# A fused attention stack: norm product in two column tiles, its least square laid on the sums in PSUM, roots spread by transfers

## The chip, the cores and the metric

One core of a Trainium2 chip runs the whole kernel in one launch. The metric is the device time of an execution in microseconds. Engines: PE is the tensor engine (PEld its weight loads), DVE the vector engine, ACT the scalar engine, POOL GpSimd, SP the engine whose queue issues the transfers.

## What is computed

The input x is (8, 256, 128) in float32. It is layer-normalised, and the result is x plus two branches of the normalised rows. The first is causal attention with 16 heads of 64. The second has six layers of local attention (window 32) and a gated MLP, and the part of it that matters here is the normalisation of queries and keys:

```python
def l2norm(t):
    return t / jnp.maximum(jnp.linalg.norm(t, axis=-1, keepdims=True), 1e-12)
...
q = l2norm(q) * qs
k = l2norm(k) * ksc
q = q * cos * scale + rotate_half(q) * sin * scale
k = k * cos * inv + rotate_half(k) * sin * inv
out = local_attention(q, k, v)
```

`qs` and `ksc` are per-channel factors, cos, sin and scale depend on the position alone. So the kernel multiplies the raw projections with tables that hold the factors and the positions, and applies 1/norm per token and head afterwards.

## The kernel before, in words

**Units, groups, slots.** A unit is one of the 8 batch rows in one of the 6 layers, so there are 48 units. Each has 4 groups of 4 heads; a group m has its place in a stream of 192 groups (`GROUPS`). The program of every engine is a loop over slots s, from -4 to a few past 192 (`slot(s)` in each engine's block), and in one slot the engines work on different groups: the projections and rotation are those of group s+4, the norm product that of s+3, the scores and softmax those of s, the weighting of the values that of s-1, the output projection that of s-2. The order within a slot is written out by hand for each engine, each engine runs it in order, and semaphores join them. The first four slots (-4 to -1) run inside the last batch of the causal branch. The MLP of two units together is spread over the slots 13 to 21 of a cycle of 8 slots (`mlp_slot`), so a slot's extra work depends on s modulo 8. Layer boundaries, every 32 slots, add weight loads, weight splits on POOL (L426, L431) and, on ACT, new rotary tables (L643).

**The norm of queries and keys.** In a slot:
- PE projects K (`keys`, L1061 to L1063, first half) and, later in the slot, Q (`queries`) of group s+4 into the banks `B_K` and `B_Q`, as three single-pass products each half.
- DVE multiplies each with the tables (`rotate`: L1376 into `rot_u`, L1377 into `rot_v`); ACT squares each (`squares`, L655 into `sq`). For Q, DVE waits until ACT has squared (it waits for `q_square`); for K, ACT waits for DVE (`k_prod`).
- POOL adds `rot_u` and the swapped `rot_v` (`rotated`, L442, into `z_raw`, one operation for K and one for Q) and the two halves of the squares (L469, into `sqs`, 128x512: K and Q by 256 tokens).
- PE multiplies `sqs` (group s+3) with the matrix `blk`, 128x128, ones where both indices lie in the same block of 32 (`norms`, L1010, 512 columns): every partition of `B_N` then holds the sum of squares of its own head. The operands are float32, which takes two passes of PE for a product, two records in the trace.
- ACT takes Ln (L735) and Exp with the scale -0.5 (L738), both 128x512, so that `rinv` is the reciprocal root, on all partitions.
- DVE clips it to 1e12 (L1458, `bound_ready`), after the softmax weights of the slot.
- POOL multiplies `z_raw` with it (`normalise`, L436, once for K and once for Q) into `z_norm`. Its order: rotated K (s+4), normalise K (s+3), sum of squares (s+4), normalise Q (s+3), rotated Q (s+4).
- SP moves `z_norm` of group s+2 into `zqk` (L365, four transfers of 128 KB) with the layout of the scores, and then part of the values into `v_late` (L371, L372, group s+3).

**The softmax and the rest of the slot.** PE makes the scores (`windows`, L1029) onto a mask that ACT (L689) or PE (L1020) has laid into `pair_bank`. DVE: maximum (L1355), shift (L1357), rotation of K (L1376, L1377), then, after ACT's Exp (L731), sum (L1362), reciprocal (L1364) and weights (L1367), then the clip L1458, then MLP products (L1419) and residuals (L1411), then the rotation of Q. In some slots it begins with L1349 (spreading), L1391 (MLP residual) or L1398 (a copy for the layer norm). ACT: values out of PSUM (L595), spreading (L664), Exp of the scores (L731), Ln and Exp of the norms (L735, L738), `yt` (L696), squares of K, pieces of layer norm and MLP (L684, L678, L702), the mask (L689), squares of Q. In the slot of remainder 1 the mask stands ahead of the squares of K. PE: transposes of the weights (L1039), scores, K projection, output projection (L978), norm product, weighting of the values (L1051, in column tiles of 64), an MLP product (L1113, L1127 or L1135), Q projection, V projection (L1073 to L1075), and in some slots products for the layer norm (L1149, L1157). The V projection overwrites `B_N`, so it waits for ACT's Ln.

Of the kernel before, what the change touches and what calls it, by code (L numbers as in the profile page):

```python
# [16 lines left out]
P = 128  # L17
# [45 lines left out]
for _name, _n in (("ident", P), ("mask_causal", P), ("mask_local", 4 * KEYS), ("blk", P),  # L63
                  ("center", P), ("avg", P), ("rot", 4 * T)):
    CONST[_name] = (_at, _n)
    _at += _n
# [3 lines left out]
def constants():  # L70
# [17 lines left out]
    put("blk", i // 32 == np.arange(P)[None, :] // 32)  # L88
# [14 lines left out]
def build(nc, x, w_kv_down, w_kv_up, w_q, w_out, Wqkv, q_scale, k_scale, Wo, ln_g, ln_b, W1, b1, W2, b2, const, out):  # L103
    with ExitStack() as ctx:
# [42 lines left out]
        z_raw = sb("z_raw", [P, 2, 2, 2, T])  # L147
        z_norm = sb("z_norm", [P, 2, 2, 2, T])
# [7 lines left out]
        x_rows = z_norm.rearrange("p g a b t -> p (g a b t)").rearrange("p (n c) -> p n c", c=P)  # L156
        xn_rows = z_raw.rearrange("p g a b t -> p (g a b t)").rearrange("p (n c) -> p n c", c=P)
# [4 lines left out]
        late_ln = probs.rearrange("p h c -> p (h c)")[:, 2 * GW * 2:].rearrange("p (a t) -> p a t", a=2)  # L162
        late_rinv = probs_t.rearrange("p h c -> p (h c)")[:, 2 * GW * 2:].rearrange("p (a t) -> p a t", a=2)
# [13 lines left out]

        def ln_n(m):

            return late_ln if m >= G else gate[:, 0:2, 0:T]  # L180

        def rinv(m):

            return late_rinv if m >= G else gate[:, 0:2, T:2 * T]
# [16 lines left out]
            n_done ln_done rinv_ready bound_ready zn_ready z_in0 z_in1 z_in2 z_in3 lv_ready v_late_in0 v_late_in1 v_late_in2 v_late_in3  # L201
# [81 lines left out]
        def _(sp):  # L283
# [72 lines left out]
            def slot(s):  # L356
                if active(s, -2, GROUPS - 2):
# [5 lines left out]
                    for pair in range(2):  # L363
                        for half in range(2):
                            sp.dma_start(zqk[half:P:2, g, :, pair, :], z_norm[64 * pair:64 * pair + 64, s % 2, :, half, :]).then_inc(S[f"z_in{g}"], 16)  # L365
                if active(s, -3, GROUPS - 3):

                    g, odd = (s + 3) % G, (s + 3) // G % 2
                    cols = slice(g * GW, (g + 1) * GW)
                    sp.wait_ge(S["lv_ready"], s + 4)  # L370
                    sp.dma_start(v_late[WIN:P, odd, :, cols], v_sb[0:P - WIN, odd, :, cols]).then_inc(S[f"v_late_in{g}"], 16)  # L371
                    sp.dma_start(v_late[0:WIN, odd, 1, cols], v_sb[P - WIN:P, odd, 0, cols]).then_inc(S[f"v_late_in{g}"], 16)  # L372
# [40 lines left out]
        def _(pool):  # L413
# [19 lines left out]
            def normalise(m, idx):  # L433

                parity = m % 2
                return pool.tensor_tensor(z_norm[:, parity, idx, :, :], rinv(m)[:, idx, :].unsqueeze(1).broadcast_to([P, 2, T]), z_raw[:, parity, idx, :, :], ALU.mult)  # L436

            def rotated(m, parity, idx, prod, mark):

                pool.wait_ge(S[prod], m + 1)  # L440
                after(pool, "zn_ready", m - 1)
                pool.tensor_tensor(z_raw[:, parity, idx, :, :], rot_u[:, idx, :, :], rot_v[:, idx, ::-1, :], ALU.add).then_inc(S[mark], 1)  # L442
# [8 lines left out]
            def slot(s):  # L451
                g = s % G
                one, two = active(s, -4, GROUPS - 4), active(s, -3, GROUPS - 3)
# [3 lines left out]
                if one:  # L457
                    rotated(s + 4, s % 2, 1, "k_prod", "k_summed")
                if two:

                    pool.wait_ge(S["bound_ready"], s + 4)
                    after(pool, f"z_in{(s + 1) % G}", 16 * HG * ((s + 1) // G + 1))
                    pool.wait_ge(S["k_summed"], s + 4)
                    normalise(s + 3, 1)
# [5 lines left out]
                if two:  # L470
# [1095 lines left out]
```

## Time and profile before

| | before |
|---|---|
| time, median of 3 runs | 1865.2 us (1863.66 to 1868.27) |
| the profiled execution's own time | 1865.6 us |
| its span, first to last instruction | 1863.8 us |
| busy: PE, DVE, ACT, POOL | 1804.9, 1531.7, 1455.7, 1359.5 us |
| mean granted clock of PE | 0.998 |
| share of 16 DMA engines, SP's queue | 35.9% |

The span is that of the profiled execution, whose own time is 1.8 us longer. Busy times overlap between engines. In a timeline row stand start, duration, engine, line, operation, output<-input, shape and count, and in brackets the idle time of the engine before it with its releaser. Starts of two neighbouring instructions on DVE and ACT lie some 0.1 us closer together than the first one's duration, so their starts, not their durations, are what adds up along a queue.

### The profile page before, as it was taken

To read this page: it belongs to the slowest core of one execution; us is meant where nothing else is said; L and a number is where in the kernel's file an instruction comes from. 1 tells how busy PE (TensorE), PEld (TensorE's weight loads), DVE (VectorE), ACT (ScalarE), POOL (GpSimd) and SP (SyncE) were. 2 spreads that over 40 slices of the span, in tenths; PEclk is the share of its full clock that TensorE was granted. 3 is DMA by queue.
4 is the path that set the end of the run, shared out by engine and by line. 5 is a ranking of instruction groups with operands and counts; after the bars stand their busy time and mean duration, and the time that the engine had idled before them with its cause. 6 is when DMAs were issued, how large, how long until landed. Compare 5 with 4: busy or idle time off the path is not lost.

```text
span 1863.8 us, 67159 instructions
## 1 busy us (share of the span) xinstructions
PE 1804.9 (97%) x26763; PEld 1367.6 (73%) x26763; DVE 1531.7 (82%) x3002; ACT 1455.7 (78%) x2976; POOL 1359.5 (73%) x1165
## 2 busy tenths in 40 slices
PE   6999998999999999999999999999999999999997
PEld 4777776777777777777777777777777777777774
DVE  5776777788889888888888888888888888888886
ACT  5766665688788878888887888878878888887884
POOL 3010033899889888888888898889888888888880
PEclk9999999999999999999999999999999999999999
DMA  3000001344444444444443444444444444444342
GB/s 111 1 1 0 0 25 38 96 123 115 101 101 115 106 112 104 100 112 103 119 110 97 104 111 111 115 107 101 105 110 109 114 99 107 112 103 100 95 106 64
DMA packets 188251, 170.91 MB, mean 92 GB/s; under 512 B 20112, under 2 KB 187192, under 8 KB 187960
## 3 DMA queue, kind: packets, MB, share of 16 engines
q1 hardware_dynamic: 187960, 166.84, 35.9%
q8 instruction: 206, 3.38, 0.8%
q14 instruction: 85, 0.70, 0.1%
HBM read 21.01 MB, written 1.05 MB: 12 GB/s over the span
## 4 chain that ended last, share of the span: by engine, by line
PE 65%; ACT 12%; DVE 11%; issue 7%; POOL 4%; DMA 0%; SPq 0%; ACTq 0%; POOLq 0%; DVEq 0%
PE bank L1010 6%; PE bank L1051 6%; PE bank L978 6%; PE pair_bank L1029 5%; PE bank L1061 4%; PE bank L1113 3%; PE bank L1062 3%; PE bank L1063 3%; PE bank L1039 3%; PE bank L1135 3%; PE bank L896 2%; ACT sq L655 2%; DVE rot_v L1377 2%; ACT probs L735 2%; DVE rot_u L1376 2%
## 5 line engine op out<-in xcount | busy, mean ns | idle before, releaser
L436 POOL TENSOR_TENSOR z_norm<-probs_t,z_raw 128x512 f32<-128x512 f32 x376 | 480.9, 1279 | 101.2 <-DVE probs_t L1458 101.2
L442 POOL TENSOR_TENSOR z_raw<-rot_u,rot_v 128x512 f32<-128x512 f32 x384 | 498.3, 1302 | 70.8 <-DVE rot_v L1377 69.6
L1376 DVE TENSOR_TENSOR rot_u<-bank,tabs 128x512 f32<-128x512 f32 x384 | 262.9, 685 | 175.9 <-ACT sq L655 174.5
L1061 PE MATMUL bank<-x_high,w_high 128*128 128x256 f32 x768 | 302.1, 393 | 0.0
L469 POOL TENSOR_TENSOR sqs<-sq 128x512 f32<-128x512 f32 x192 | 246.3, 1283 | 60.5 <-issue 59.3
L1377 DVE TENSOR_TENSOR rot_v<-bank,tabs 128x512 f32<-128x512 f32 x384 | 261.1, 680 | 0.0
L1051 PEld LDWEIGHTS bank<-probs_t,v_late 128*64 128x64 f32 x3072 | 155.0, 137 | 144.5 <-issue 144.5
L655 ACT ACTIVATE sq<-bank 128x512 f32<-128x512 f32 x384 | 222.1, 593 | 24.1 <-PE bank L1063 17.7
L731 ACT ACTIVATE pair_bank<-pair_bank 128x512 f32<-128x512 f32 x192 | 111.7, 582 | 165.0 <-DVE pair_bank L1357 163.4
L664 ACT ACTIVATE probs_t<-bank 64x512 f32<-64x512 f32 x340 | 200.8, 591 | 22.7 <-PE bank L1039 20.7
L1063 PE MATMUL bank<-x_low,w_high 128*128 128x256 f32 x768 | 216.3, 282 | 0.0
L1062 PE MATMUL bank<-x_high,w_low 128*128 128x256 f32 x768 | 216.1, 281 | 0.0
L1010 PE MATMUL bank<-sqs,consts 128*128 128x512 f32 x384 | 197.6, 596 | 9.9 <-POOL sqs L469 9.9
L1051 PE MATMUL bank<-probs_t,v_late 128*64 128x64 f32 x3072 | 198.8, 228 | 0.5 <-ACT probs_t L664 0.5
L978 PE MATMUL bank<-yt,wo 128*128 128x256 f32 x768 | 197.8, 380 | 0.0
L1051 PE MATMUL bank<-probs_t,v_sb 128*64 128x64 f32 x3072 | 189.5, 222 | 0.0
L1061 PEld LDWEIGHTS bank<-x_high,w_high 128*128 128x128 f32 x768 | 144.6, 188 | 58.0 <-issue 38.5
L1062 PEld LDWEIGHTS bank<-x_high,w_low 128*128 128x128 f32 x768 | 145.8, 190 | 36.9 <-issue 36.9
L735 ACT ACTIVATE probs<-bank,tiny 128x512 f32<-128x512 f32 x188 | 129.1, 686 | 43.6 <-PE bank L1010 41.9
L1029 PE MATMUL pair_bank<-zqk 64*32 64x64 f32 (+1 forms) x12288 | 161.4, 221 | 0.9
L1051 PEld LDWEIGHTS bank<-probs_t,v_sb 128*64 128x64 f32 x3072 | 156.0, 138 | 0.0
L1029 PEld LDWEIGHTS pair_bank<-zqk 64*32 64x32 f32 x12288 | 130.6, 105 | 34.7 <-issue 34.7
(190 smaller groups left out, 4533.9 us busy)
## 6 DMA issues: line engine op xcount, KB each, us to landing
zqk<-z_norm SPq DMA_DIRECT2D x768, 128.0 KB
v_late<-v_sb SPq DMA_DIRECT2D x192, 192.0 KB, 2.6
w_stage<-in_L_ffn_Wqkv SPq DMA_DIRECT2D x24, 384.0 KB, 3.6
v_late<-v_sb SPq DMA_DIRECT2D x192, 32.0 KB, 2.2
wo<-in_L_ffn_Wo SPq DMA_DIRECT2D x24, 128.0 KB, 2.4
w<-in_L_ffn_W SPq DMA_DIRECT2D x12, 170.5 KB, 2.7
z_norm<-in_L_attn_x SPq DMA_DIRECT2D x4, 256.0 KB, 5.0
out<-z_raw SPq DMA_DIRECT2D x4, 256.0 KB, 2.3
```

The lines of the kernel that those rows point to most:

```text
L436: return pool.tensor_tensor(z_norm[:, parity, idx, :, :], rinv(m)[:, idx, :].unsqueeze(1).broadcast_to([P, 2, T]), z_raw[:, parity, idx, : ...
L442: pool.tensor_tensor(z_raw[:, parity, idx, :, :], rot_u[:, idx, :, :], rot_v[:, idx, ::-1, :], ALU.add).then_inc(S[mark], 1)
L655: act.activation(sq[:, idx, :, :], src[:, :].rearrange("p (a t) -> p a t", a=2), ACT.Square).then_inc(S[mark], 1)
L978: mm = pe.matmul(B_X[:, 0:T], wo[:, c, :], yt[:, c, :], start=(c == 0), stop=(c == HD // P - 1))
L1010: pe.matmul(B_N[:, :], con("blk"), sqs[:, :, :].rearrange("p a t -> p (a t)"), start=True, stop=True).then_inc(S["n_done"], 1)
L1029: mm = pe.matmul(bank[a][WIN * tile:WIN * tile + WIN, at + skip:at + KEYS], zqk[rows, g, 0, pair, WIN * j:WIN * j + WIN], zqk[rows, g, 1, ...
L1051: mm = pe.matmul(y[:, t, tile % 2, :, :], (v_sb if tile % 2 else v_late)[:, odd, t, f], spread[:, h, tile, :], start=True, stop=True, tile ...
L1061: pe.matmul(dst, w_high[:, r, j, cols], x_high[:, odd, :], start=True, stop=False)
L1062: pe.matmul(dst, w_low[:, r, j, cols], x_high[:, odd, :], start=False, stop=False)
L1063: mm = pe.matmul(dst, w_high[:, r, j, cols], x_low[:, odd, :], start=False, stop=True)
L1376: dve.tensor_tensor(rot_u[:, idx, :, :], src, tabs[:, 2 * idx, :, :], ALU.mult)
L1377: dve.tensor_tensor(rot_v[:, idx, :, :], src, tabs[:, 2 * idx + 1, :, :], ALU.mult).then_inc(S[mark], 1)
```

## The change

It has four parts.
- **The norm product** gives each head's sum on 16 partitions instead of 32: `blk` is 128x64, and two products of 256 columns put K's or Q's sums on partitions 0 to 63 (the first, idx 0, which is Q) and 64 to 127 (the second, K) of the first 256 columns of `B_N`, in two column tiles of PE (`tile_position` (0, 0) and (0, 64)).
- **The least square**: DVE lays max(sum, 1e-24) on the sums in `B_N`, in place, 128x256, in place of the clip of the root. It stands in DVE's slot right after the rotation of K, ahead of the softmax weights, and waits for the norm product. ACT's Ln waits for it. Ln and Exp run over 128x256.
- **The root is spread by transfers**: a new group of four transfers by SP writes the 64 rows of each root to all 128 partitions of a buffer `wide` (every second partition, twice, for Q and for K; 64 KB each). They stand at the head of SP's slot behind the `v_late` transfers, which move ahead of the `z` transfers.
- **Normalising** happens a slot later (group s+2 instead of s+3), in place in one buffer `z` of four groups, which replaces `z_raw` and `z_norm`. POOL's order is now: rotated K (s+4), normalise K and Q (s+2), sum of squares (s+4), rotated Q (s+4). The transfers into `zqk` still leave in slot s for group s+2.

```diff
-    put("blk", i // 32 == np.arange(P)[None, :] // 32)
+    put("blk", i // 32 == np.arange(P // 2)[None, :] // 16)
...
-        z_raw = sb("z_raw", [P, 2, 2, 2, T])
-        z_norm = sb("z_norm", [P, 2, 2, 2, T])
+        z = sb("z", [P, G, 2, 2, T])
...
+        def wide(m):
+            return (late_wide if m >= G else early_wide)[:, m % 2, :, :]
...
@@ SP, slot(s) @@
+                if active(s, -3, GROUPS - 3):
+                    g, odd = (s + 3) % G, (s + 3) // G % 2
+                    cols = slice(g * GW, (g + 1) * GW)
+                    sp.wait_ge(S["lv_ready"], s + 4)
+                    sp.dma_start(v_late[WIN:P, odd, :, cols], v_sb[0:P - WIN, odd, :, cols]).then_inc(S[f"v_late_in{g}"], 16)
+                    sp.dma_start(v_late[0:WIN, odd, 1, cols], v_sb[P - WIN:P, odd, 0, cols]).then_inc(S[f"v_late_in{g}"], 16)
+                    sp.wait_ge(S["rinv_ready"], s + 4)
+                    after(sp, "zn_ready", s + 2)
+                    for idx in range(2):
+                        for k in range(2):
+                            sp.dma_start(wide(s + 3)[k:P:2, idx, :], rinv(s + 3)[64 * idx:64 * idx + 64, :]).then_inc(S[f"wide_in{(s + 3) % 2}"], 16)
                 if active(s, -2, GROUPS - 2):
...
-                            sp.dma_start(zqk[half:P:2, g, :, pair, :], z_norm[64 * pair:64 * pair + 64, s % 2, :, half, :]).then_inc(S[f"z_in{g}"], 16)
-                if active(s, -3, GROUPS - 3):
...
+                            sp.dma_start(zqk[half:P:2, g, :, pair, :], z[64 * pair:64 * pair + 64, g, :, half, :]).then_inc(S[f"z_in{g}"], 16)
...
@@ POOL @@
+                zs = z[:, m % G, idx, :, :]
+                return pool.tensor_tensor(zs, wide(m)[:, idx, :].unsqueeze(1).broadcast_to([P, 2, T]), zs, ALU.mult)
...
-                after(pool, "zn_ready", m - 1)
+                after(pool, f"z_in{m % G}", 16 * HG * (m // G))
...
-                if two:
-
-                    pool.wait_ge(S["bound_ready"], s + 4)
-                    after(pool, f"z_in{(s + 1) % G}", 16 * HG * ((s + 1) // G + 1))
-                    pool.wait_ge(S["k_summed"], s + 4)
-                    normalise(s + 3, 1)
+                if near:
+                    pool.wait_ge(S[f"wide_in{s % 2}"], 16 * HG * ((s + 2) // 2 + 1))
+                    pool.wait_ge(S["k_summed"], s + 3)
+                    normalise(s + 2, 1)
+                    pool.wait_ge(S["q_summed"], s + 3)
+                    normalise(s + 2, 0).then_inc(S["zn_ready"], 1)
...
@@ ACT @@
-                    act.wait_ge(S["n_done"], m + 1)
-                    act.activation(ln_n(m), B_N[:, :].rearrange("p (a t) -> p a t", a=2), ACT.Ln, bias=tiny[:, 0:1], scale=LNS).then_inc(S["ln_done"], 1)
+                    act.wait_ge(S["bound_ready"], m + 1)
+                    after(act, f"wide_in{m % 2}", 16 * HG * (m // 2))
+                    act.activation(ln_n(m), B_N[:, 0:T], ACT.Ln, bias=tiny[:, 0:1], scale=LNS).then_inc(S["ln_done"], 1)
...
-                    after(act, "zn_ready", m)
...
@@ PE @@
-                pe.matmul(B_N[:, :], con("blk"), sqs[:, :, :].rearrange("p a t -> p (a t)"), start=True, stop=True).then_inc(S["n_done"], 1)
+                for idx in range(2):
+                    rows = slice(64 * idx, 64 * idx + 64)
+                    mm = pe.matmul(B_N[rows, 0:T], con("blk"), sqs[:, idx, :], start=True, stop=True, tile_position=(0, 64 * idx), skip_group_check=True)
+                mm.then_inc(S["n_done"], 1)
...
@@ DVE, slot(s) @@
                     rotate(s + 4, 1, B_K, "lk_done", "k_summed", "k_prod")
+                if two:
+                    dve.wait_ge(S["n_done"], s + 4)
+                    dve.tensor_scalar(B_N[:, 0:T], B_N[:, 0:T], 1e-24, None, ALU.max).then_inc(S["bound_ready"], 1)
...
                     weigh_down(s)
-                if two:
-                    dve.wait_ge(S["rinv_ready"], s + 4)
-                    dve.tensor_scalar(rinv(s + 3), rinv(s + 3), 1e12 / ROOT, None, ALU.min).then_inc(S["bound_ready"], 1)
```

## Rows read from the trace of the kernel before

**Rows 1.** Page, part 1: busy time and share of the span.
```profile
PE 1804.9 (97%) x26763; PEld 1367.6 (73%) x26763; DVE 1531.7 (82%) x3002; ACT 1455.7 (78%) x2976; POOL 1359.5 (73%) x1165
```

**Rows 2.** Timeline of PE: scores of slots 16, 96, 99, 100, 104, 184.
```profile
448.75 0.68 PE L1029 MATMUL pair_bank<-zqk 64*32 64x32 f32 x47
...
1084.48 0.84 PE L1029 MATMUL pair_bank<-zqk 64*32 64x32 f32 x64
...
1107.10 0.84 PE L1029 MATMUL pair_bank<-zqk 64*32 64x32 f32 x64
...
1114.91 0.84 PE L1029 MATMUL pair_bank<-zqk 64*32 64x32 f32 x64
...
1147.18 0.84 PE L1029 MATMUL pair_bank<-zqk 64*32 64x32 f32 x64
...
1780.34 0.68 PE L1029 MATMUL pair_bank<-zqk 64*32 64x32 f32 x48
```

**Rows 3.** Timeline of DVE, slot 103 (r = 7).
```profile
1139.00 0.69 DVE L1376 TENSOR_TENSOR rot_u<-bank,tabs 128x512 f32<-128x512 f32 x1 [1.50 <-ACT sq L655]
...
1140.20 0.41 DVE L1398 COPY xc<-bank 128x256 f32<-128x256 f32 x1
1140.54 0.68 DVE L1355 TENSOR_REDUCE nm<-pair_bank 128x8 f32<-128x512 f32 x1
...
1142.46 0.68 DVE L1377 TENSOR_TENSOR rot_v<-bank,tabs 128x512 f32<-128x512 f32 x1
...
1144.00 0.69 DVE L1367 TENSOR_TENSOR probs<-pair_bank,rrec 128x512 f32<-128x512 f32 x1
...
1147.03 0.69 DVE L1376 TENSOR_TENSOR rot_u<-bank,tabs 128x512 f32<-128x512 f32 x1 [2.00 <-ACT sq L655]
```

**Rows 4.** Timeline of PE around one norm product.
```profile
1007.11 1.02 PE L1010 MATMUL bank<-sqs,consts 128*128 128x512 f32 x2
...
1008.07 0.34 PE L1051 MATMUL bank<-probs_t,v_late 128*64 128x64 f32 x4
...
1009.15 1.12 PE L1113 MATMUL bank<-xh,w 128*128 128x512 f32 x2
```

**Rows 5.** Groups by line, 700 to 1400 us: count, busy, mean, idle.
```profile
L1458 DVE TENSOR_SCALAR probs_t<-probs_t 128x512 f32<-128x512 f32 x88 | 49.9, 567 | 0.0
...
L670 ACT ACTIVATE ln_v<-bank,tiny 128x256 f32<-128x256 f32 x22 | 10.4, 474 | 0.6
```

**Rows 6.** Timeline of ACT, slot 103 (r = 7).
```profile
1142.80 0.69 ACT L735 ACTIVATE probs<-bank,tiny 128x512 f32<-128x512 f32 x1 [0.24 <-PE bank L1010]
...
1144.06 0.58 ACT L696 ACTIVATE yt<-bank 128x512 f32<-128x512 f32 x1
...
1145.02 0.41 ACT L684 ACTIVATE xc<-xc 128x256 f32<-128x256 f32 x1
1145.32 0.68 ACT L702 ACTIVATE gate<-bank,gate_bias 85x512 f32<-85x512 f32 x1
1145.89 0.59 ACT L689 ACTIVATE pair_bank<-mask_local_b 128x512 f32<-128x512 bf16 x1
1146.41 0.59 ACT L655 ACTIVATE sq<-bank 128x512 f32<-128x512 f32 x1
```

**Rows 7.** Timeline of DVE, slots of remainder 1, 2, 5.
```profile
900.92 1.38 DVE L1349 COPY probs_t<-bank 64x512 f32<-64x512 f32 x2
...
1105.17 0.74 DVE L1419 SCALAR_TENSOR_TENSOR hid<-bank,out_bias,gate 128x512 f32<-128x512 f32 x1
...
1124.83 1.51 DVE L1391 SCALAR_TENSOR_TENSOR xs<-bank,out_bias,xs 64x512 f32<-64x512 f32 x2
```

**Rows 8.** Timeline of ACT, slot 100 (r = 4): squares of Q.
```profile
1122.99 0.60 ACT L655 ACTIVATE sq<-bank 128x512 f32<-128x512 f32 x1 [1.27 <-PE bank L1063]
```

**Rows 9.** Timeline of SP, slot 100: a group's `z` and values.
```profile
1116.93 3.48 SPq L365 DMA_DIRECT2D zqk<-z_norm  x4
1120.46 0.64 SPq L371 DMA_DIRECT2D v_late<-v_sb  x1
```

More of the change, by code:

```diff
@@ L62 @@
 _at = 0
-for _name, _n in (("ident", P), ("mask_causal", P), ("mask_local", 4 * KEYS), ("blk", P),
+for _name, _n in (("ident", P), ("mask_causal", P), ("mask_local", 4 * KEYS), ("blk", P // 2),
                   ("center", P), ("avg", P), ("rot", 4 * T)):
@@ L153, in build @@
         nm = sb("nm", [P, HG, TT])
-        x_rows = z_norm.rearrange("p g a b t -> p (g a b t)").rearrange("p (n c) -> p n c", c=P)
-        xn_rows = z_raw.rearrange("p g a b t -> p (g a b t)").rearrange("p (n c) -> p n c", c=P)
+        z_rows = z.rearrange("p g a b t -> p (g a b t)").rearrange("p (n c) -> p n c", c=P)
+        x_rows, xn_rows = z_rows[:, 0:NB * TT, :], z_rows[:, NB * TT:2 * NB * TT, :]
         probs = sb("probs", [P, HG, 3 * P])
@@ L176, in build @@
         causal_stage = [w_stage] + [a.rearrange("p (j n) -> p j n", j=3) for a in (hid_flat[:, 0:3 * GW], hid_flat[:, 3 * GW:6 * GW], gate_flat[:, 0:3 * GW])]
+        early_wide = gate_flat[:, 0:4 * T].rearrange("p (q a t) -> p q a t", q=2, a=2)
+        early_rows = gate_flat[:, 4 * T:6 * T].rearrange("p (q t) -> p q t", q=2)
         def ln_n(m):
-            return late_ln if m >= G else gate[:, 0:2, 0:T]
+            return rinv(m)
         def rinv(m):
-            return late_rinv if m >= G else gate[:, 0:2, T:2 * T]
+            return (late_rows if m >= G else early_rows)[:, m % 2, :]
+        def wide(m):
+            return (late_wide if m >= G else early_wide)[:, m % 2, :, :]
         pair_bank = ctx.enter_context(nc.psum_tensor("pair_bank", [P, 2, 512], F32))
@@ L433, in normalise, with rotated @@
             def normalise(m, idx):
-                parity = m % 2
-                return pool.tensor_tensor(z_norm[:, parity, idx, :, :], rinv(m)[:, idx, :].unsqueeze(1).broadcast_to([P, 2, T]), z_raw[:, parity, idx, :, :], ALU.mult)
-            def rotated(m, parity, idx, prod, mark):
+                zs = z[:, m % G, idx, :, :]
+                return pool.tensor_tensor(zs, wide(m)[:, idx, :].unsqueeze(1).broadcast_to([P, 2, T]), zs, ALU.mult)
+            def rotated(m, idx, prod, mark):
                 pool.wait_ge(S[prod], m + 1)
-                after(pool, "zn_ready", m - 1)
-                pool.tensor_tensor(z_raw[:, parity, idx, :, :], rot_u[:, idx, :, :], rot_v[:, idx, ::-1, :], ALU.add).then_inc(S[mark], 1)
+                after(pool, f"z_in{m % G}", 16 * HG * (m // G))
+                pool.tensor_tensor(z[:, m % G, idx, :, :], rot_u[:, idx, :, :], rot_v[:, idx, ::-1, :], ALU.add).then_inc(S[mark], 1)
             def split_input(unit, b, odd):
@@ L452, in slot @@
                 g = s % G
-                one, two = active(s, -4, GROUPS - 4), active(s, -3, GROUPS - 3)
+                one, near = active(s, -4, GROUPS - 4), active(s, -2, GROUPS - 2)
                 if s == 0:
@@ L469, in slot @@
                     pool.tensor_tensor(sqs[:, :, :], sq[:, :, 0, :], sq[:, :, 1, :], ALU.add).then_inc(S["sums_ready"], 1)
-                if two:
-                    pool.wait_ge(S["q_summed"], s + 4)
-                    normalise(s + 3, 0).then_inc(S["zn_ready"], 1)
-                if one:
-                    rotated(s + 4, s % 2, 0, "q_prod", "q_summed")
+                    rotated(s + 4, 0, "q_prod", "q_summed")
                 if g == 0 and active(s, -4, GROUPS - 8):
@@ L1455, in slot @@
                     weigh_down(s)
-                if two:
-                    dve.wait_ge(S["rinv_ready"], s + 4)
-                    dve.tensor_scalar(rinv(s + 3), rinv(s + 3), 1e12 / ROOT, None, ALU.min).then_inc(S["bound_ready"], 1)
                 if s == 0:
```

13 lines of the change are left out of this document (4 added, 9 removed).

## The prediction

> **What bounds the kernel now.** I read first the busy shares: TensorE (PE) is busy for 1804.9 of 1863.8 us, 97%, the vector engine (DVE) for 82%, ScalarE (ACT) for 78%, POOL for 73% [rows 1]. Then the starts of the score matmuls (L1029) give the length of slots; I number slots by their remainder r by 8, since the MLP comes round every 8. One such group of 8 slots without a layer boundary takes 1147.18 - 1084.48 = 62.70 us; slots 16 to 184 take 1331.6 us, 63.41 per group, so layer boundaries add 0.71 per group, 14.9 us over the 21 groups [rows 2]. PE's timeline has hardly a gap inside a slot. DVE and ACT do wait: in a slot of r = 7 DVE stands idle 2.00 us until the squares of Q are done [rows 3]. So PE is the bound, and the question is how much slack the ring between DVE and ACT has, since the change lengthens it.
>
> **Part 1: norm product in two column tiles.** The product with `blk` (L1010) takes PE from 1007.11 to 1008.07, 0.96 us for two passes of 512 columns; of this I take 0.10 for the change to column tiles behind it (an estimate), 0.43 for a pass [rows 4]. The new one has 256 columns in each of two tiles. Nearest rows: the 32 passes of L1051, 64 columns each in tiles of 64, go in 1.08 us (1008.07 to 1009.15), 34 ns a pass [rows 4]. At L1010's rate (0.43 us for 512 columns) one pass of 64 columns takes 54 ns, so two tiles run side by side. Then the four new passes of 256 take 2 x 0.215 = 0.43 us instead of 0.86; the 0.10 of the change to column tiles moves ahead of the product and stays. PE gives back 0.43 us a slot. Bounds: 0.43 and 0 (tiles one after the other). The Trainium skill has a rule against it: TensorE: Matmul & The Clock Gate, Part 3 (The mechanism), says that a weight load overlaps matmuls in flight only where the row group differs, and the two tiles here share all rows. By that rule the product would keep near its 0.86 us and the time be the 1895 of rival B; L1051's tiles share their rows too and do overlap, so the row speaks against the rule.
>
> **Part 2: the bound (1e-24) laid on the sums by DVE, before ACT's Ln.** Today ACT goes from its Exp of the scores straight to Ln (it needs the norm product alone), and DVE's bound (L1458, mean 567 ns [rows 5]) comes after the softmax weights. The new bound is a 128x256 operation on PSUM; the nearest row, the 128x256 copy out of PSUM (L1398), took 0.41 and the next instruction started 0.34 after it [rows 3]. I take 0.34 for it in the queue; L1458's mean for 512 columns in SBUF [rows 5] gives both ends, half of it and the whole: 0.28 and 0.57, less the same 0.07 of overlap 0.21 and 0.50. The page VectorE: DVE Perf Modes, Why PSUM operands drop a tier (the Trainium skill), says that fp32 with a PSUM operand runs at the plain rate; L1398 agrees, and by it the low end falls away.
> ACT's Ln and Exp shrink to half the width: from Ln's start to the start of `yt` was 1144.06 - 1142.80 = 1.26 [rows 6]; a Ln of 128x256 took 474 ns [rows 5], 0.50 to the next start, and an ACT operation of 128x256 (L684) took 0.41, of which 0.33 is queue: 0.83.
> But Ln now waits for DVE, in whose queue stand the reduce of the scores, the shift, the two K rotations, and then the bound. Take N, the start of the reduce L1355 at 1140.54. The second K rotation ends at 1142.46 + 0.68 = 1143.14, N+2.60 [rows 3]; the bound ends at N+2.94, Ln starts at N+2.98 and `yt` at N+3.81. Without the wait Ln would follow the scores' Exp. Queued behind Ln on ACT stand Exp, `yt`, squares of K, MLP pieces, the mask and the squares of Q; for the last DVE waits before it rotates Q, and behind that stands the next slot's reduce. That closes the ring.
>
> **Its length.** After `yt` starts ACT needs, at r = 7, 1147.00 - 1144.06 = 2.94 until the squares of Q end; of this L684 is 0.30, the gate bias L702 0.57, the mask L689 0.52, the last squares 0.59 [rows 6]. Without MLP pieces Q = 2.07, without the mask too 1.55. Then 0.03 to DVE's rotation of Q and 1.20 until DVE is free for the next [rows 3]. A step from N to the next N is so 3.81 + Q + 1.23 + E = 5.04 + Q + E; E is what DVE does first: 0.34 for L1398 (r = 3, 7), 1.41 for the two L1349 (r = 1), 1.54 for the two L1391 (r = 5) [rows 3, 7].
> - r = 0: 5.04 + 1.55 + 1.41 = 8.00.
> - r = 1: the mask comes before the squares and needs the softmax weights, at N + 2.94 + 1.55 = 4.49 (L1367 ends 1.55 after the rotation [rows 3]): 4.53 + 0.52 + 0.48 + 0.59 + 1.23 + 0 = 7.36.
> - r = 5: 7.11. r = 6: 5.04 + 2.64 + 0.34 = 8.02. r = 7: 5.04 + 2.94 = 7.98.
> - r = 2 to 4: here PE is in the chain. The hidden product (L1419) ends at N + 4.49 + 0.67 = 5.16; from its end to the score matmuls of r = 3 is 1107.10 - 1105.91 = 1.19; that slot takes PE 7.81 - 0.43 = 7.38 [rows 2, 7]; from the scores of r = 4 to the end of the squares of Q, behind the down-projection, 1123.59 - 1114.91 = 8.68, less 0.43 = 8.25 [rows 2, 8]; then 0.03 + 1.20 + 1.54. Sum 24.75. (The ring alone would give 24.0.)
> Together 63.22 us against 62.70, while PE's own work falls to 62.70 - 8 x 0.43 = 59.3. In the old order `yt` started at 1144.06 - 1140.54 = N+3.52, and that with ACT waiting for PE's product ahead of Ln, so the ring was 0.3 us a slot shorter or more and stood hidden behind PE. Over 21 groups +0.52 makes +10.9 us.
>
> **The rest.** Layer boundaries: the old 14.9 us came in good part from L1458 held up while POOL splits weights (its mean of 567 ns is above L1398's 0.41 [rows 3, 5]), with POOL's norm behind it; the new bound is in PSUM and POOL no longer waits for it, so I drop them. In their place the rotary tables (L643) stand in ACT's queue before the squares: two and some small copies at r = 3, four at r = 4, each 128x256 as L684 with its 0.41 [rows 6], an estimate of 1.1 and 1.6 us. Of these 2.7 PE's lead at the down-projection (8.25 against the ring) hides 0.7; the stretch r = 2 to 4 grows by 2.0, x 5 layers = +10. Weight splits on POOL ahead of `sqs` and the bias copy: an estimate of 0.6 a layer, +3. The first 16 slots have a ring with few extras: +2. POOL keeps its five operations (73% busy in all [rows 1]) and stays hidden while slots keep their length; its sum of squares comes one operation later, and without that cover PE's product would be late. SP issues per slot two `v_late`, the four new transfers of 64 KB and four `z`, in that order. One issue takes 0.64, ten 6.4; the four `z` took 3.48, so 0.9 of stall [rows 9], together 7.3 of 7.9 us: hidden, with 0.6 to spare; if that goes, rival C. The norms a slot later, in place, cost nothing: the `z` transfers leave in the same slot as before, the rest is waits met long ago.
> Sum: +10.9 - 14.9 + 10 + 3 + 2 = +11 on the profiled execution's own 1865.6 us (span 1863.8), which is 0.4 above the median: **1877 us**.
>
> **Rivals.** A (the other side): PE stays the bound, and its 0.43 x 192 = 82 us come out: 1784. For it: PE is at 97% and DVE and ACT show idle time [rows 1, 3]. Against it: that idle time is the slack that the new wait uses up. It decides if the ring is under 59.3 a group, 0.5 us less in each slot than I sum; anything between scales (0.3 less would give 1827). Chance 0.15.
> B: the tiles don't overlap. The two 0.43 in the stretch r = 2 to 4 are then not saved: 0.86 x 21 = +18, 1895. Chance 0.10.
> C: SP becomes the bound: if the new transfers show the stall of 0.9 too, SP needs 8.2 a slot, 65.6 a group, +50 and more; where only some slots do, 1890 to 1930. Chance 0.13.
> My forecast, the DVE-ACT ring: 0.62. Its own range comes from the bound, which stands six times in a group: 0.13 less each is -16, 0.16 more +20, which the rest doesn't add to in full, and rounding of some 40 terms, +/-8: 1857 to 1897.
>
> **Numbers.** A measurement of this kernel can tell about 0.3%, 5.6 us, from no change. The range takes in the forecast's, B and the lower part of C: 1855 to 1905; left out are A and half of C. Faster: A and a little of the forecast's low end, 0.19. Same: 0.18 of the forecast. Slower: the rest, 0.63.
>
> **What would show it.** After: slots of some 7.9 us as before; PE's busy share down to about 94%; its norm product 0.43 us; PE waiting ahead of the scores and the mask; Ln (L735 before) with about 0.9 us idle before it, released by the bound; DVE still waiting for the squares. Wrong, if slots shrink to 7.4 with PE closed up (A), if the product takes 0.86 (B), or if `z` or the roots land late (C).

## The result and the profile after

The changed kernel takes **1894.12 us** (median of 4 runs, 1893.61 to 1895.13) against 1864.68 (median of 4 runs of before on the same chip, 1863.66 to 1868.27): ratio 1.0155, 95% interval 1.0137 to 1.0173. The forecast was 1877 us with a range of 1855 to 1905: slower as forecast, but by 29 us where the sum gave 11 (12 against the median of before). The profiled execution has a span of 1892.8 us against 1863.8.

First the page: part 1 and the chain that ended last (part 4).

```profile
PE 1755.7 (93%) x27147; PEld 1362.9 (72%) x27147; DVE 1528.6 (81%) x3002; ACT 1371.9 (72%) x2976; POOL 1354.5 (72%) x1165
...
DVE 34%; PE 32%; ACT 14%; issue 11%; SPq 5%; DMA 1%; POOL 1%; ACTq 0%; DVEq 0%
```

PE went from 97% [rows 1] to 93%, and the chain is no longer PE's: DVE holds a third of it, and PE's share fell from 65% to 32%. The waits name the ring (the engine that waits and its line, the line waited for: us in total, times, longest):

```profile
DVE rot_u L1386 <- ACT sq L662: 212.8, 146, 2.5
...
ACT probs_t L743 <- DVE bank L1464: 168.8, 187, 0.9
...
PE pair_bank L1039 <- DMA zqk<-z: 8.2, 12, 1.3
```

ACT's Ln (L743) waits 0.9 us in nearly every slot for DVE's bound (L1464), and DVE waits for ACT's squares of Q. PE's waits for `z` are small. The starts of the score matmuls (L1039; slots 0, 16, 96, 104, 184), to set beside [rows 2]:

```profile
338.78 0.84 PE L1039 MATMUL pair_bank<-zqk 64*32 64x32 f32 x64
...
460.38 0.81 PE L1039 MATMUL pair_bank<-zqk 64*32 64x32 f32 x62
...
1103.30 0.85 PE L1039 MATMUL pair_bank<-zqk 64*32 64x32 f32 x64
...
1166.93 0.85 PE L1039 MATMUL pair_bank<-zqk 64*32 64x32 f32 x64
...
1809.25 0.84 PE L1039 MATMUL pair_bank<-zqk 64*32 64x32 f32 x64
```

A group of 8 slots without a layer boundary takes 63.63 us (1166.93 - 1103.30), 62.70 before. Slot 0 of before, which the rows ahead of the prediction lack, starts so:

```profile
332.01 1.11 PE L1029 MATMUL pair_bank<-zqk 64*32 64x32 f32 x64
```

So the 29.0 us by which the span grew divide into **start** 338.78 - 332.01 = +6.8; **first 16 slots** 121.60 against 116.74 = +4.9; **slots 16 to 184** 1348.87 against 1331.59 = +17.3; behind them +0.1.

One slot of r = 0 (slot 104). Timeline of DVE, answering to [rows 3]:

```profile
1170.51 0.42 DVE L1464 TENSOR_SCALAR bank<-bank 128x256 f32<-128x256 f32 x1
1170.84 1.39 DVE L1413 TENSOR_TENSOR xc<-xc,rstd 128x256 f32<-128x256 f32 x1
1172.16 0.68 DVE L1372 TENSOR_REDUCE rsum<-pair_bank 128x8 f32<-128x512 f32 x1
...
1173.71 0.68 DVE L1386 TENSOR_TENSOR rot_u<-bank,tabs 128x512 f32<-128x512 f32 x1
```

Timeline of POOL in the same slot:

```profile
1170.67 1.28 POOL L453 TENSOR_TENSOR z<-rot_u,rot_v 128x512 f32<-128x512 f32 x1 [1.25 <-DVE rot_v L1387]
1171.91 2.68 POOL L447 TENSOR_TENSOR z<-probs,z 128x512 f32<-128x512 f32 x2
```

Timeline of ACT there, answering to [rows 6]:

```profile
1170.97 0.47 ACT L743 ACTIVATE probs_t<-bank,tiny 128x256 f32<-128x256 f32 x1 [0.95 <-DVE bank L1464]
...
1172.28 1.07 ACT L662 ACTIVATE sq<-bank 128x512 f32<-128x512 f32 x2
```

Timeline of PE around the product, answering to [rows 4]:

```profile
1169.48 0.65 PE L1019 MATMUL bank<-sqs,consts 128*64 128x256 f32 x4
1169.97 0.28 PE L1061 MATMUL bank<-probs_t,v_late 128*64 128x64 f32 x4
```

The bound takes 0.33 us in the queue (1170.51 to 1170.84; I took 0.34). The next instruction is the product that gives the MLP's normed rows (L1413, "the late norms" below; L1403 before). It takes 1.39 us; in most slots of before it took 0.41 (mean of all 1269 ns, 610 before). POOL had started its K sum (L453) 0.17 us before it, and the product ends 0.28 us after that operation (1171.95). Of the 48 of these products in each of the two kernels, every one that began while a POOL operation ran ends 0.28 to 0.31 us after that operation. In most slots of before either no POOL operation ran there, or one that ended some 0.12 us after the product's start, and so it took 0.41. The squares of Q are done at 1173.35, but DVE comes to the rotation of Q only at 1173.71.

### The profile page after: what moved, and what is told of

Its sections match the earlier page's. It is cut to its first block, busy times and chain, and to the rows that moved or that the text cites. A ratio compares the mean times of both kernels' runs of the same rounds, so it can differ in the third digit from the quotient of the medians.

```text
span 1892.8 us, 68880 instructions
## 1 busy us (share of the span) xinstructions
PE 1755.7 (93%) x27147; PEld 1362.9 (72%) x27147; DVE 1528.6 (81%) x3002; ACT 1371.9 (72%) x2976; POOL 1354.5 (72%) x1165
## 4 chain that ended last, share of the span: by engine, by line
DVE 34%; PE 32%; ACT 14%; issue 11%; SPq 5%; DMA 1%; POOL 1%; ACTq 0%; DVEq 0%
DVE rot_u L1386 9%; DVE rot_v L1387 9%; ACT sq L662 5%; DVE nm L1365 5%; DVE bank L1464 3%; ACT yt L703 2%; PE bank L1145 2%; SPq L383 2%; ACT pair_bank L696 2%; PE bank L1061 2%; PE bank L903 2%; ACT probs_t L743 2%; PE bank L985 2%; SPq L374 2%; DVE rsum L1372 2%
## 5 line engine op out<-in xcount | busy, mean ns | idle before, releaser
L453 POOL TENSOR_TENSOR z<-rot_u,rot_v 128x512 f32<-128x512 f32 x384 | 491.0, 1279 | 234.6 <-DVE rot_v L1387 234.6
L447 POOL TENSOR_TENSOR z<-probs,z 128x512 f32<-128x512 f32 x376 | 480.8, 1300 | 3.6 <-DMA probs<-probs_t 3.5
L743 ACT ACTIVATE probs_t<-bank,tiny 128x256 f32<-128x256 f32 x188 | 89.1, 474 | 168.8 <-DVE bank L1464 168.8
L985 PE MATMUL bank<-yt,wo 128*128 128x256 f32 x768 | 197.7, 380 | 0.0
L1061 PEld LDWEIGHTS bank<-probs_t,v_late 128*64 128x64 f32 x3072 | 173.3, 138 | 33.1 <-issue 9.3
L1061 PE MATMUL bank<-probs_t,v_late 128*64 128x64 f32 x3072 | 190.7, 222 | 1.8 <-ACT probs_t L671 1.6
L1039 PE MATMUL pair_bank<-zqk 64*32 64x64 f32 (+1 forms) x12288 | 165.1, 221 | 17.6 <-ACT pair_bank L696 9.4
L1039 PEld LDWEIGHTS pair_bank<-zqk 64*32 64x32 f32 x12288 | 134.5, 105 | 53.3 <-issue 40.7
L1049 PE MATMUL bank<-consts,probs 128*128 128x128 f32 x768 | 117.9, 276 | 31.1 <-DVE probs L1377 29.3
```

Of the source, the lines that this page charges most:

```text
L447: return pool.tensor_tensor(zs, wide(m)[:, idx, :].unsqueeze(1).broadcast_to([P, 2, T]), zs, ALU.mult)
L453: pool.tensor_tensor(z[:, m % G, idx, :, :], rot_u[:, idx, :, :], rot_v[:, idx, ::-1, :], ALU.add).then_inc(S[mark], 1)
L985: mm = pe.matmul(B_X[:, 0:T], wo[:, c, :], yt[:, c, :], start=(c == 0), stop=(c == HD // P - 1))
L1039: mm = pe.matmul(bank[a][WIN * tile:WIN * tile + WIN, at + skip:at + KEYS], zqk[rows, g, 0, pair, WIN * j:WIN * j + WIN], zqk[rows, g, 1, ...
L1061: mm = pe.matmul(y[:, t, tile % 2, :, :], (v_sb if tile % 2 else v_late)[:, odd, t, f], spread[:, h, tile, :], start=True, stop=True, tile ...
```

## The experiments

Two theories stand against each other: **R**, the ring between DVE and ACT through the bound sets the pace; **C**, SP's ten issues a slot and the transfers behind them do. The recorded expectations call C also "S" or "SP theory", and P stands there for PE as the bound. Where nothing else is said, line numbers are the changed kernel's. Each run stands beside runs of before on its chip, medians 1864.25 to 1865.78.

### The order alone

The kernel before, with `B_N` bounded at full width behind the rotation of K, Ln waiting for it, and the clip of the root (L1458 before) gone: no transfers, no column tiles.

> The kernel before with one part of the change alone: DVE lays max(sum, 1e-24) on the sums in PSUM right after the rotation of K, here over all 512 columns, and ACT's Ln waits for it; the clip of the root is left out. Full-width product, Ln and Exp, no new transfers, the norms in their old slot. Theory R (the ring between DVE and ACT sets the length of a slot): the bound takes about 0.60 us of DVE's queue and Ln with Exp 1.26, so a step of the ring is 5.73 us + Q + E instead of 5.04 + Q + E, a group of 8 slots 67 to 69 us, and the time 1960 to 2010 us. Rival S (the cost lies in the transfers, SP's queue and the norms a slot later): none of these is here, the time stays near 1865, at most 1875 us. Rival P (PE is the bound and the tiles are the cause): near 1865 too.

**2003.57 us** (one run), a group 68.3 us, both as R had them. The bound in this place, at double width, makes the old kernel 139 us slower with not one transfer more.

### The old clip put back

In short form (Ln waits for the product alone again):

```
-  dve: wait n_done; B_N[:, 0:T] = max(B_N[:, 0:T], 1e-24)     (ahead of Ln)
+  dve: wait rinv_ready; rinv = min(rinv, 1e12 / ROOT)         (behind the weights; SP waits for it)
```

> The changed kernel with that one part undone: Ln waits for the norm product alone, and DVE clips the root (now 128x256) after the softmax weights, as before the change; SP's transfers of the root wait for the clip. Tiles, half width, transfers and the norms a slot later stay. R: the ring is back under PE's work, a group takes 59.3 to 60 us, the time is 1780 to 1800 us, and Ln has hardly any idle time before it that DVE ends. S: the transfers and the moved norms are still there, so it stays at 1880 or above. P (the tiles save PE nothing): about 1865 us.

**1913.18 us**, ratio 1.0253 (1.0233 to 1.0272). For R, which gave 1780 to 1800, that is a miss of over 110 us; C had 1880 or above. Its groups between slots 16 and 184 are irregular, 64.2 to 67.4 us. The chain of its page:

```profile
PE 32%; DVE 32%; SPq 12%; issue 12%; ACT 6%; DMA 5%; POOL 1%; ACTq 0%; DVEq 0%
```

One of its waits (total, times, longest; in the changed kernel it was 12.3 us in 17 times):

```profile
PEld pair_bank L1039 <- DMA zqk<-z: 43.9, 67, 3.1
```

Its clip, by form (count, busy, mean ns, idle before): late slots, then the first four:

```profile
L1468 DVE TENSOR_SCALAR probs_t<-probs_t 128x256 f32<-128x256 f32 x188 | 219.0, 1165 | 3.4 <-ACT probs_t L745 3.4
L1468 DVE TENSOR_SCALAR gate<-gate 128x256 f32<-128x256 f32 x4 | 1.6, 406 | 1.6 <-ACT gate L745 1.6
```

With the ring open two costs show at once. The clip, both sides in SBUF, takes 1165 ns on the mean. POOL, which in the old order waited for it, now works beside it: 183 of the 192 clips last over 0.5 us, and each of them began during a POOL operation and ends 0.14 to 0.16 us after it. The seven that began with POOL idle took 0.28 us (three of the first four, whose mean of 406 ns holds one late one). And SP waits for the clip, then issues late; `z` lands late, and PE waits. R is not refuted, but C stands right behind it.

### The product twice; the first four groups free

```
-  for idx in range(2):            (L1019, norm product)
+  for idx in (0, 1, 0, 1):
```

> The changed kernel with the norm product issued twice (four column-tile products instead of two, same result). The added 0.43 us of PE in each slot: under R PE is in the chain only in the stretch from remainder 2 to 4, for two slots of it, so a group grows by 0.86 us and the time by 18 to 24 us, to 1912 to 1918. If PE were the bound everywhere, by 0.43 x 192 = 82 us, to 1976. If nothing of PE were in the chain, by nothing. If the tiles ran one after the other, the product would add 0.86 a slot, 36 us or more under R.

**1910.37 us** (one run), +16; a group 64.5 us, 0.8 more. It lies just under R's 1912 to 1918, and far from the 1976 of a PE that is the bound everywhere: 0.8 us a group is the added product in two slots of eight, which fits the prediction's stretch r = 2 to 4.

```
-  if two:                         (bound of DVE)
+  if two and s + 3 >= G:
```

and Ln of the first four groups waits for the product alone: this kernel leaves out their least square.

> The changed kernel, but in the first four groups (those worked on inside the last batch of the causal branch) Ln waits for the product alone and their least square is left out. R: there PE's V projection waits up to 3.6 us four times, since Ln waits for a bound that stands in DVE's queue behind the causal softmax; with it gone the first scores of the local attention start at about 332 us instead of 338.8, PE's granted clock from 300 to 340 us is back above 0.9 from 0.79, and the time is 6 to 8 us less, about 1887. S: no difference beyond 2 us, since the transfers stay.

**1890.94 us** (one run), -3.2, where 6 to 8 less were expected. The start came back whole: first scores at 331.0 instead of 338.8. The rest of the run lost some 4 us again (steady groups 63.9, not 63.6; ACT has one more wait in each slot, the likely reason, not tested). The clock shows what had happened at the start. Windows, changed kernel; columns: window, its length, busy us of PE, PEld, DVE, ACT, POOL, mean granted clock of PE, DMA share and GB/s:

```profile
300.00:320.00 20.00, 12.72 (x80) 9.22 (x81) 11.33 (x33) 9.37 (x33) 5.17 (x5) 0.77 0.10 26
320.00:340.00 20.00, 16.36 (x159) 11.71 (x158) 10.71 (x29) 9.64 (x29) 11.73 (x10) 0.80 0.35 83
```

and this run:

```profile
300.00:320.00 20.00, 15.73 (x116) 10.56 (x114) 13.84 (x40) 12.54 (x42) 9.02 (x8) 1.00 0.16 41
320.00:340.00 20.00, 17.23 (x183) 12.70 (x188) 12.32 (x28) 8.47 (x24) 12.00 (x11) 0.91 0.37 90
```

In the changed kernel PE stands idle for 3.64 us before its V projection three times (0.78 to 0.93 in the kernel before), and the granted clock has a mean of 0.77 and 0.80 of the full 2.4 GHz in the two stretches, so PE ran part of them at the lower level, 1.2 GHz. In this run two waits of 0.71 are left of them, and the clock is 1.00 and 0.91, as in the kernel before. The row is the changed kernel's:

```profile
319.45 0.58 PE L1083 MATMUL bank<-w_high,x_high 128*128 128x256 f32 x1 [3.64 <-ACT gate L743]
```

### The bound ahead of the rotation of K; the late norms ahead of the bound

Only the order of DVE's blocks is changed in each.

> The changed kernel, with the bound on the sums put ahead of DVE's rotation of K instead of behind it (nothing left out). Ring theory: Ln then starts about 0.9 us earlier after the reduce of the scores, so the ring is shorter than PE's work (some 60 us for a group of 8 slots); without another bound the time falls to 1795 to 1830 us, PE's share of the span rises over 95%, and Ln waits no more than about 0.3 us a slot. SP theory: with that wait gone, the issue of ten transfers a slot and the stall of each (some 7.3 to 8.2 us a slot) sets the pace: 1840 to 1885 us, with PE waiting for zqk from the transfers as in the run with the clip put back. If neither: the rotation of K, now later, delays POOL and the squares of K, and the time stays at 1885 to 1900.

**1897.31 us**, ratio 1.0174 (1.0153 to 1.0194): the third case. Its DVE:

```profile
614.37 0.70 DVE L1367 TENSOR_TENSOR pair_bank<-pair_bank,nm 128x512 f32<-128x512 f32 x1
616.01 0.43 DVE L1462 TENSOR_SCALAR bank<-bank 128x256 f32<-128x256 f32 x1 [0.94 <-PE bank L1019]
616.35 0.68 DVE L1386 TENSOR_TENSOR rot_u<-bank,tabs 128x512 f32<-128x512 f32 x1
```

The norm product stands behind the scores, the K projection and L985 in PE's order and ends 3.0 us into the slot. The bound then waits 0.94 for it with the rotation of K, the sums and the softmax weights queued behind. In this slot Ln starts 2.83 us after the scores' reduce, 2.98 in the changed kernel, and the sums (L1372) 3.90 after it, 2.86 there: little gained for Ln, 1.0 lost for the rest. As means of slots 16 to 184 Ln gains 0.59 and the sums lose 0.31. The rotation of K had filled that wait of DVE. The loss comes back in the ring, for ACT's mask now waits for the softmax weights (7.8 us in all in the changed kernel):

```profile
ACT pair_bank L696 <- DVE probs L1377: 100.0, 140, 1.5
```

> The changed kernel with one thing moved: the product that gives the normed rows (1.40 us in the slots of remainder 0 and 4, 0.41 in the kernel before) stands ahead of the bound instead of behind it. If it is long because POOL's rotated K holds the SBUF port just then, it goes back to about 0.4 us, and the bound then comes 0.4 later: the step of slot r = 0 stays near 8.3 us, and the time within 6 us of the changed kernel (1888 to 1900). If it is long by its own form, it stays at 1.4 us and delays the bound: +1 us in two slots of 8, 1915 us and more.

**1899.89 us** (one run); the product fell to a mean of 480 ns (1269 in the changed kernel), steady group 63.7. As expected (1888 to 1900), and no gain: 0.33 of bound and product change places in the ring. So it is not long by its own form. (The 6 us more lie in the first 16 slots, 127.9 us against 121.6; their cause is open.)

### Without the bound

> The changed kernel with the least square left out: Ln waits for the norm product alone. Ring theory: the ring between DVE and ACT is open, and PE is the bound again with 0.48 us less a slot: 1784 to 1805 us. SP theory: ten transfers a slot set the pace, 1840 to 1885 us, with waits of PE for zqk. The difference between this run and the one with the bound first is what the bound costs when it is early: by the ring theory under 15 us.

**1838.48 us**, ratio 0.9859 (0.9838 to 0.988). So the bound costs 56 us in all, and taking it away makes the kernel 26 us faster than before. But it doesn't reach PE's 1784 to 1805: what is left is C's, just under the 1840 that it gave.

> The changed kernel with the least square as the bias of ACT's Ln (sum + 1e-24 in place of the larger of the two; Ln had a bias already) and DVE's instruction gone: no instruction is left for the bound and Ln waits for the norm product alone. It has the schedule of the run without a bound, so every theory gives that run's time: 1832 to 1845 us. If it differs, Ln's time depends on the bias.

The edit: `tiny[:, 0:1]` = LNS * 1e-24 (2^-64 before), which Ln adds to LNS times the sum. **1840.93 us**, ratio 0.9882 (0.9865 to 0.99), as expected. Its chain:

```profile
PE 37%; SPq 32%; DVE 10%; ACT 7%; issue 7%; DMA 4%; POOL 2%; ACTq 0%; DVEq 0%
```

and its SP in one slot, from one L368 to the next, 7.92 us, of which issues take 7.69:

```profile
612.94 0.64 SPq L368 DMA_DIRECT2D v_late<-v_sb  x1
613.62 0.62 SPq L369 DMA_DIRECT2D v_late<-v_sb  x1
614.34 2.46 SPq L374 DMA_DIRECT2D probs<-probs_t  x4
616.84 3.97 SPq L383 DMA_DIRECT2D zqk<-z  x4
620.86 0.64 SPq L368 DMA_DIRECT2D v_late<-v_sb  x1
```

Four new transfers take 2.46, the four `z` 3.97, so 1.5 us of stall in this slot (3.07 and 0.6 in the one before). This is a full slot; as a mean of slots 16 to 184 the ten issues take 6.9 us (6.0 to 8.9) of 7.7.

> The kernel before with its bound moved in the same way (bias of Ln, DVE's L1458 gone, POOL's normalise waits for the root alone). PE is the bound there at 97%: inside a group nothing changes; DVE's held up L1458 at the layer boundaries goes, worth at most the 15 us that they add: 1850 to 1863 us. If the bound held the old kernel back elsewhere too, under 1845.

**1844.80 us**, ratio 0.9895 (0.988 to 0.9909): below what I expected. PE holds 85% of the chain, and the steady group is 62.2 us, not 62.7: in the old kernel too, DVE's clip held up the hidden product in the slots of r = 2 (8.46 us, now 8.00). So most of what the version with the bound as a bias gains has nothing to do with this change: the two differ by 4 us, with intervals that overlap. What PE gives back with 0.48 us a slot is not seen in the time, since SP's queue is next (see the added issue below).

### Who issues, and how often

> As the run with the bound ahead of the rotation of K, and besides the four transfers that spread the root are issued on ACT's queue instead of SP's, right behind the Exp that makes the root (ACT waits there for its own Exp to be written, and issues four). SP theory: SP is free of four of ten issues and of the wait for the root, so if SP was the bound, the time falls by 20 us or more against that run. Ring theory: ACT's four issues (an estimate of 0.05 to 0.6 us each in its queue) stand between the Exp and the square root pieces of the next slot; at 0.6 each the ring is 2.4 us longer and the time goes over 1950; at 0.1 each it stays within 15 us of that run.

**2360.33 us**, ratio 1.267. That is over 1950, as R had it for long issues: four of them take ACT 2.41 us, in the ring. Against the run with the bound first it is 463 us more, and 192 x 2.41 is 463 too; PE's mean granted clock is 0.92 here, and what that adds was not parted from it.

```profile
800.18 2.41 ACTq L745 DMA_DIRECT2D probs<-probs_t  x4
802.69 0.60 ACT L698 ACTIVATE yt<-bank 128x512 f32<-128x512 f32 x1 [2.54 <-issue]
```

> As the run with the bound as a bias, and in SP's slot the four transfers of the root stand ahead of the two v_late instead of behind them. SP theory (the z transfers land late because SP comes late to them: the root is ready at 4.2 us of a slot, but SP first waits for V and issues the four from 6.3 us on): they leave from about 4.3 us on, z leaves up to 1.4 us earlier, PE's waits for zqk from DMA (some 50 us in all) mostly go, and the time falls by 20 to 50 us to 1790 to 1820. If SP is bound by the sum of its issues (7.3 us a slot with the stall), the order changes nothing: 1830 to 1845. If v_late becomes the late one, PE waits for v_late instead: 1840 and more.

**1852.49 us**, ratio 0.993 (0.9917 to 0.9944): not the gain, and 12 us slower than with the old order. It lies in the third range (1840 and more), but not for that reason: PE waits for no `v_late`. SP now waits for the root 87 us in all (24 with the roots behind `v_late`), its count of issues stays, and PE's waits for `z` go from 42.5 to 57.8 us.

```
-  v_late[32:128] <- v_sb[0:96]                   (L368, one transfer)
+  v_late[32:80] <- v_sb[0:48]; v_late[80:128] <- v_sb[48:96]
```

> The changed kernel with the 192 KB transfer of v_late cut in two of 96 KB: one issue more on SP in each slot, the same bytes. Ring theory (SP has some room left): SP waits 0.36 us a slot for the root and now and then for z, so of the 0.62 us of an issue at most 0.3 shows: 0 to +30 us, 1894 to 1925. If SP already sets the pace (rival C): +0.62 us in each of 190 slots, +90 to +120: 1985 and more.

> The same cut in the kernel with the bound as a bias of Ln (1841 us). SP theory, in which the issues of SP are now the bound (32% of its chain): +0.62 us in most slots, +70 to +120: 1910 to 1960. If DVE, ACT and PE bound it and late transfers are only an accident of order: +0 to +25.

**1953.03** (+59 on the changed kernel, ratio 1.0468) and **1944.77** (+104 on the kernel with the bias, ratio 1.0426). The second is C as expected. The first lies between the two ranges: spread over 190 slots, 0.31 of the 0.62 us shows, so SP had about 0.3 us a slot of room in the changed kernel, half of the 0.6 that I had summed. With 11 issues both kernels come out within 8 us of each other, where the bound parted them by 53; the first one's chain:

```profile
SPq 39%; PE 23%; DVE 16%; ACT 9%; issue 9%; DMA 3%; POOL 1%; ACTq 0%; DVEq 0%
```

> The kernel with the bound as a bias of Ln (1841 us), and the 32 KB transfer of v_late issued by POOL, at the end of its slot, instead of by SP: nine issues a slot on SP. SP theory: adding an issue there cost 104 us; with one less SP has some 0.6 us a slot of room, PE's waits for zqk go and PE or the DVE-ACT ring is the bound: 1790 to 1815 us. If POOL's issue is long (over 1 us; nothing so far shows it), POOL, busy 6.4 us of a slot of 7.5, becomes the bound: over 1841. If the late transfers come from the DMA engines and not from SP's issue, nothing changes: 1830 to 1845.

**1860.48 us**, ratio 0.9978 (0.9968 to 0.9988): inside none of the expected ranges but "over 1841", and POOL's issue is not long (0.54 us), as that one had assumed. SP is free now (it waits 226 us for root and `z`) and steady groups take 60.2 us, but most second slots of r = 4 take some 11.6 us, with the late norms' product (L1417 here) held up by POOL. DVE in slot 28:

```profile
553.88 5.23 DVE L1417 TENSOR_TENSOR xc<-xc,rstd 128x256 f32<-128x256 f32 x1
```

POOL in the same slot, its issue (L484) among them:

```profile
553.30 1.27 POOL L452 TENSOR_TENSOR z<-rot_u,rot_v 128x512 f32<-128x512 f32 x1
554.52 0.54 POOL L484 DMA_DIRECT2D v_late<-v_sb  x1
555.08 1.27 POOL L452 TENSOR_TENSOR z<-rot_u,rot_v 128x512 f32<-128x512 f32 x1
556.30 2.51 POOL L446 TENSOR_TENSOR z<-probs,z 128x512 f32<-128x512 f32 x2
```

The product starts 0.58 us after the first of these and ends 0.30 us after the last (558.81), so DVE got in between none of them. Eleven of the 48 products are held for 5.2 to 6.0 us in this run. It is not the issue on POOL that does it alone: in the run without the bound one of 48 took 4.88 us, with the roots first one took 5.03, beside POOL operations that follow each other without an issue.

Next, rstd (the reciprocal root for the late norms) goes to PSUM, in short form; PE's next writers of that bank `B_M` wait for the product instead of Ln:

```
-  act: rstd (SBUF) = exp(-0.5 ln_v);            dve: xc = xc * rstd
+  act: B_M[:, T:2T] (PSUM) = exp(-0.5 ln_v);    dve: xc = B_M[:, T:2T] * xc
```

> The kernel with nine issues on SP and one on POOL, and besides rstd of the late norms is written to the free half of B_M in PSUM, so that DVE's product xc x rstd has one operand in PSUM. In the run before, its steady groups took 60.2 us, but one instruction, that product with both operands in SBUF, was held up to 5.2 us while POOL ran four operations in a row, and so one slot in 8 or 16 took 11.6. If POOL's hold on the SBUF operands is the cause, the product takes 0.4 to 0.45 us everywhere, the slots of 11.6 become 8.7, and the time is 1800 to 1825 us. If it is POOL's lateness itself that costs (the product of norms waits for POOL's sums), the long slots stay and the time is 1845 and more.

> The kernel with the bound as a bias of Ln (ten issues on SP, 1841 us), with rstd in PSUM in the same way. SP sets the pace there: 1830 to 1845 us. If the held up product was part of it: under 1825.

With nine issues on SP **1824.76 us**, ratio **0.9777** (0.9764 to 0.9791): the fastest of all, 41 us under before. With ten **1838.44** (0.9863), in the range that SP as the bound gave, and no clear gain on the same kernel without rstd in PSUM (0.9882). The two differ only in who issues the 32 KB transfer, so these 13.7 us are SP's issue and not the bytes. The product takes 416 ns in both:

```profile
L1417 DVE TENSOR_TENSOR xc<-bank,xc 128x256 f32<-128x256 f32 x46 | 19.1, 416 | 0.0
```

With an operand in PSUM the wait is gone; PE holds 57% of the chain with nine issues. Of the slots of r = 4 with 11.6 us half became 8.7 and half 9.7; PE waits 35.2 us in all for POOL's sums there, so POOL itself is late now and then.

## Why the forecast was slower as measured, and too small

**What held.** PE was the bound and no longer is; the ring took its place. Ln starts 2.98 us after N (the start of the scores' reduce) and `yt` 3.81, both as summed. From N to N the steps of slots 96 to 103 are 8.33, 7.38, 24.80, 7.12, 8.02, 7.98 for r = 0, 1, 2 to 4, 5, 6, 7, against 8.00, 7.36, 24.75, 7.11, 8.02, 7.98: five of six to 0.05 us. Rival A is out: a group takes 63.63 us, where the prediction had left PE 59.3 of work. Rival B is out: from the product's start to the next line are 0.48 us (2.55 to 3.03 into the slot) where it was 0.96, so the tiles run side by side though they share all rows. The Trainium skill, TensorE: Matmul & The Clock Gate, Part 3 (The mechanism), says that a weight load overlaps products in flight only where the row group differs. I had read from it a product that stays near 0.86; the 0.48 measured decides against that.

Layer boundaries add 1348.87 - 21 x 63.63 = 12.6 us; I had 13, and its main term held for its reason: at a boundary the steps of r = 3 and 4 are 8.54 and 10.73 us instead of 7.42 and 9.93, together +1.9 for the 2.0 of the rotary tables. Rival C did not decide, but was nearer than its 0.6 us of room said: 0.3. The time lies inside the 1857 to 1897 that I gave the ring, but those bounds stood for a bound of another length and for rounding. The bound came at 0.33 for 0.34, and what is missing is of another kind, so that it fits is luck.

**The steps that failed**, terms of the sum that were too small or missing:
- *The step of r = 0, 5.04 + 1.55 + 1.41 = 8.00.* It lets DVE wait for the squares of Q. The size of the bound was right (0.34 for 0.33), but the bound moved the next instruction of r = 0 and 4, the product of the late norms, into POOL's K sum: 1.39 us instead of 0.41. At r = 0 this makes DVE 0.36 late for the squares of Q: 8.33. With the few hundredths of the other steps that is 63.63 against 63.22, +8.6 over 21 groups. At r = 4 PE's down-projection hides it. I had counted what the bound costs in the queue and not what its neighbours run beside.
- *The start*, put at nothing without a reason: +6.8. The ring begins four slots before the late slots do, while DVE has the last causal batch in its queue; the bound stands behind it, PE's V projection waits 3.64 us three times and the granted clock falls in part of that stretch. Freeing four groups gave it back whole. The three waits are 10.9 us, 2.5 before, enough for it by themselves; what the clock adds was not parted.
- *The first 16 slots*: +4.9 for +2. Here PE's score products wait for `z` (7.3 us over nine waits, none before); how much of the 4.9 that is, no run told.
- *The layer boundaries*: 12.6 for 13, -0.4.

6.8 + 2.9 + 8.6 - 0.4 = 17.9, and 11 + 17.9 = 28.9 of the measured 29.0.

**Of before I had this wrong**: that outside the boundaries its clip cost nothing. With the bound as a bias the old kernel is 20 us faster; 0.46 us of each group is the clip at r = 2, some 10 us.

**Still open**: what SP's stall of 0.6 to 1.5 us a slot is; why DVE got in between two POOL operations each time in the changed kernel but stood through four or five of them in eleven slots of the run with an issue on POOL; how the cost of the clip put back divides between its two causes, the held clip and SP's late issues.

## What to carry to other kernels

- A small operation on the path between two engines costs what stands ahead of it in its queue, not its own 0.4 us. Look first whether an instruction that runs anyway can take it in (here the bias of Ln, 53 us less).
- When an engine is relieved, measure the next bound by adding a unit of it: one transfer cut in two told SP's room, 0.3 us a slot in one kernel and next to none in the other, where the busy shares said nothing.
- After any move in DVE's order, read each neighbour's duration again, and beside what it runs. Here the instructions that read and write SBUF alone stretched when a POOL operation was under way.

## What the runs showed of the hardware that I had not expected

- DVE's 128x256 product with both inputs in SBUF took 0.41 us alone, 1.39 when a POOL operation had begun 0.17 before it (it ends 0.28 after POOL's), and 5.23 beside four POOL operations and an issue in a row; with one input in PSUM 0.42 in all 46 cases. The clip, 128x256 from SBUF to SBUF with one input, took 0.28 us alone and a mean of 1.17 beside POOL. The Trainium skill, SBUF — State Buffer, Who interferes with whom, says that whoever of the two starts first holds a shared port pair for the whole instruction; the 0.41, 1.39 and 0.42 agree, but 5.23 is more than one instruction's hold.
- An issue costs its engine some 0.62 us on SP, 0.60 on ACT and 0.54 on POOL; SP's ten issues with their stalls take a mean of 6.9 us a slot and up to 8.9 (the kernel with the bound as a bias).
- Two column tiles over the same rows run side by side: the norm product took 0.96 us as two passes of 512 columns and 0.48 as four passes of 256 in two tiles, where the columns passed in sequence would be the same.
